# First batch of a graph-network kernel reordered: W ahead of the second adj, x in four buffers, c products behind W products

## The chip, the cores and the metric

One core of a Trainium2 chip runs the whole program. The metric is the device time of one execution in microseconds (us); lower is better. Each matmul engine (TensorE, PE), vector engine (VectorE, DVE), activation engine (ScalarE, ACT), GpSimd (POOL) and SyncE (SP, which issues every DMA here) runs its own list of instructions in program order; they wait for each other on semaphores.

## The reference, cut to what matters

For each of 16 batches x is 512 nodes by 128 features, adj is 512 by 512, and there are seven relations: adj twice, a node shift, the transposes of these three, and the identity.

```python
h = jnp.maximum(_layernorm(x, axis=-1), 0.0)
A_fwd = [A1, A2, shifted]
A_list = A_fwd + [jnp.swapaxes(a, 1, 2) for a in A_fwd]
A_list.append(eye)
A = jnp.stack(A_list, axis=0)
HW = jnp.einsum('bnf,rfo->rbno', features, W[:, :F]) + jnp.einsum('rd,rdo->ro', W_edges, W[:, F:])[:, None, None, :]
AHW = jnp.einsum('rbnm,rbmo->rbno', A, HW)
out = jnp.max(AHW, axis=0) + b
x = x + _L0_gnn_ref(h, adj, adj, L0_gnn_W, L0_gnn_W_edges, L0_gnn_b)
```

A1 and A2 are both adj. `shifted` rolls a stack of identities along its batch axis, which leaves each the identity, so relations 2, 5 and 6 act on h as it is. In the kernel they are the products of h with W (H_RELS), relations 3 and 4 the products with gT (AT_RELS), and 0 and 1 the products with g (A_RELS).

## The kernel before, in words

Everything is held transposed, 128 features or outputs on the partitions and 512 nodes along the row. Per batch b the kernel

- takes the statistics of x and makes rstd and shift on DVE (`variance`, `scale_and_shift`) and h on ACT (`make_h`, L387);
- multiplies h with adj and with its transpose, both loaded from memory, into the PSUM banks bank_gT (`aggregate_T`, L673 to L682) and bank_g (`aggregate`, L691 to L699). Two of four chunks are plain fp32; for the other two, adj is split into a high part (ACT, L358, L371) and a low part (DVE, `a_lo` L504, `aT_lo` L511);
- turns h and the row sums of adj on PE (`turn_h` L640, `turn_sums` L648). The sums come from ACT's accumulators and go through POOL (`part_sums`, L282, L286);
- splits gT, hT and g into high parts (ACT) and low parts (DVE, L527, L522, L532);
- makes seven products with W, each in three passes, high by high, low by high and high by low (`product`, L736 to L738). Products 3 to 6 start from the product of the row sums with c, the relations' constant rows (`begin_products`, L714, here called the c products);
- takes the maximum over the seven: ACT begins it (`begin_best`), DVE takes six more (`take_best`, L545 for products 1 and 2, L548 for 3 to 6);
- adds x and bias on POOL (`add_bias` L295, "x+bias" in the prediction; `finish` L303) and stores.

W is split once: high parts in two casts on DVE (products 0 to 2 L577, products 3 to 6 L593), low parts on POOL (L322, L325). `NH` is 3, the number of h products.

All tiles of a batch are double-buffered, x too. The order of the work is written out by hand on each engine. DVE in batch b goes through: variance of b+2, aT_lo of b, shift of b+1, a_lo of b+1, gT_lo, hT_lo, h_lo of b+1, g_lo, six bests. In batch 0 this row stands apart (L590 to L602). SP issues all DMAs from one queue: in the loop over b first x of b+2, then adj of b+2, the store of b-1, adjT and xT of b+2. Loads into a buffer in use wait for its last reader:

```python
            def load_x(b):
                q = b % 2
                if b >= 2:
                    sp.wait_ge(h_ready, b - 1)
```

PE goes through batch 0 in lines L740 to L757 and through the others in L758 to L767. The first product of a batch waits for hT_lo, the third for the copied row sums, the c products for g_lo, `aggregate` for the last best of the batch before (its bank_g is read there).

Of the kernel before, what the change touches and what calls it, by code (L numbers as in the profile page):

```python
# [11 lines left out]
P = 128  # L12
# [13 lines left out]
WARM_UP = 10  # L26


def gnn_kernel(nc: bass.Bass, x: bass.AP, xT: bass.AP, adj: bass.AP, adjT: bass.AP, W: bass.AP,
# [14 lines left out]
    with ExitStack() as ctx:  # L44
# [13 lines left out]
        x_sb = pair("x_sb", [P, C, F])  # L58
# [3 lines left out]

# [8 lines left out]
        aT_lo = pair("aT_lo", [P, NS, N], F32R)  # L71
        summed = pair("summed", [P, 2, C, N], mybir.dt.bfloat16)
# [54 lines left out]
        x_in = [sem(f"x_in{i}") for i in range(2)]  # L127
# [73 lines left out]
        def _(sp):  # L201
            def load_x(b):
                q = b % 2
                if b >= 2:
                    sp.wait_ge(h_ready, b - 1)
                    sp.wait_ge(h0_scaled, 1)
                sp.dma_start(x_sb[q][:, :, :], x_dram[b]).then_inc(x_in[q], 16)
# [36 lines left out]
            for c in range(C):  # L244
                sp.dma_start(adjT_sb[0][:, c, :], adjT_dram[0][:, c, :]).then_inc(adjT0_in[c], 16)
                if c == 1:
                    sp.dma_start(w_sb[:, 0:1, :], w_dram[:, 2:3, :]).then_inc(wh_in, 16)
                    sp.dma_start(w_sb[:, 1:3, :], w_dram[:, 5:7, :]).then_inc(wh_in, 16)
            load_x(1)
            load_adj(1)  # L250
            sp.dma_start(w_sb[:, 3:5, :], w_dram[:, 3:5, :]).then_inc(wa_in, 16)
            sp.dma_start(w_sb[:, 5:7, :], w_dram[:, 0:2, :]).then_inc(wa_in, 16)
            load_adjT(1)
            sp.dma_start(bias_sb[:, :], biasT).then_inc(bias_in, 16)
            load_xT(0)
# [18 lines left out]
        def _(pool):  # L274
# [66 lines left out]
        def _(act):  # L341
# [290 lines left out]
        def _(pe):  # L632
# [70 lines left out]
            def begin_products(b):  # L703
# [4 lines left out]
                for i in range(NH, NPROD - int(b == B - 1)):  # L708
                    begin_product(i, bank_of[i])

            def begin_product(i, to, nodes=slice(0, N)):
                group = ORDER_A.index(ORDER[i])
                rows = slice(group * GROUP, (group + 1) * GROUP)
                nc.tensor.matmul(to[:, nodes], c_rows[rows, :], sumsT[rows, nodes], start=True, stop=False)  # L714

            def product(b, i, nodes=slice(0, N), to=None):
                r = ORDER[i]
                dst = (to or bank_of[i])[:, nodes]
# [8 lines left out]
                if i == 3:  # L727
                    pe.wait_ge(gTlo_ready, b + 1)
                    pe.wait_ge(wlo_ready, 2)
                if r in H_RELS:  # L730
                    hi, lo = hT_hi, hT_lo
                elif r in AT_RELS:
                    hi, lo = gT_hi, gT_lo
                else:
                    hi, lo = g_hi, g_lo
                nc.tensor.matmul(dst, w_hi[:, i, :], hi[:, nodes], start=(r in H_RELS), stop=False)  # L736
                nc.tensor.matmul(dst, w_lo[:, i, :], hi[:, nodes], start=False, stop=False)  # L737
                nc.tensor.matmul(dst, w_hi[:, i, :], lo[:, nodes], start=False, stop=True).then_inc(prod_psum, 1)  # L738
# [12 lines left out]
            for i in range(NH):  # L751
                if i == 2:
                    turn_sums(0)
                product(0, i)
            begin_products(0)
            for i in range(NH, NPROD):
                product(0, i)  # L757
# [11 lines left out]
            for nodes, to in zip(HALVES, last_banks):  # L769
                begin_product(NPROD - 1, to, nodes)  # L770
# [28 lines left out]
```

## Time and profile before

| | us |
|---|---|
| median of 3 runs | 230.85 |
| lowest and highest | 229.27, 233.23 |
| the profiled execution | 230.21 |
| its span, first to last instruction | 228.5 |

The profile shows when each instruction ran in one execution. PE is the matmul engine; PEclk is the clock granted to it in tenths of full speed, where 5 is 1.2 GHz and 10 (shown as 9) is 2.4 GHz. Ends of matmuls are modelled: consecutive matmuls overlap in the listing, and their starts tell the pace. An instruction's idle time before it stands in brackets with what released it; "issue" means that nothing the profile shows was waited for.

### The profile page before, as it was taken

To read this page: it belongs to the slowest core of one execution; us is meant where nothing else is said; L and a number is where in the kernel's file an instruction comes from. 1 tells how busy PE (TensorE), PEld (TensorE's weight loads), DVE (VectorE), ACT (ScalarE), POOL (GpSimd) and SP (SyncE) were. 2 spreads that over 40 slices of the span, in tenths; PEclk is the share of its full clock that TensorE was granted. 3 is DMA by queue.
4 is the path that set the end of the run, shared out by engine and by line. 5 is a ranking of instruction groups with operands and counts; after the bars stand their busy time and mean duration, and the time that the engine had idled before them with its cause. 6 is when DMAs were issued, how large, how long until landed. Compare 5 with 4: busy or idle time off the path is not lost.

```text
span 228.5 us, 3306 instructions
## 1 busy us (share of the span) xinstructions
PE 213.9 (94%) x872; PEld 145.1 (63%) x872; DVE 172.2 (75%) x414; ACT 159.0 (70%) x431; POOL 57.8 (25%) x109
## 2 busy tenths in 40 slices
PE   7973799999999899999999999999999998999994
PEld 7532466667676567667667667677666665667672
DVE  3453987697876887897779788797778869787845
ACT  3756928778686777969586877969686867966220
POOL 3106322303232231213223231213223231223200
PEclk9997589999999999999999999999999999999999
DMA  5999907759293955949393866939393966610101
GB/s 184 310 355 371 336 5 243 265 192 303 44 382 103 313 185 200 308 100 331 114 346 127 264 241 209 295 123 348 88 333 123 306 202 238 221 46 3 47 0 46
DMA packets 31586, 47.13 MB, mean 206 GB/s; under 512 B 1632, under 2 KB 11088, under 8 KB 31568
## 3 DMA queue, kind: packets, MB, share of 16 engines
q1 hardware_dynamic: 31568, 46.92, 61.4%
q8 instruction: 7, 0.11, 0.2%
q14 instruction: 11, 0.09, 0.1%
HBM read 42.72 MB, written 4.19 MB: 205 GB/s over the span
## 4 chain that ended last, share of the span: by engine, by line
PE 85%; SPq 5%; DMA 4%; DVE 2%; issue 2%; DVEq 0%
PE bank_g L691 12%; PE bank_p L736 12%; PE bank_gT L673 11%; PE bank_p L738 10%; PE bank_p L737 10%; DMA x_sb<-in_x_dram 4%; PE bank_p L714 3%; PE bank_g L695 3%; PE bank_gT L678 3%; PE bank_gT L679 3%; PE bank_g L696 3%; PE bank_g L699 3%; PE bank_gT L682 3%; PE bank_p L640 3%; PE bank_p L648 3%
## 5 line engine op out<-in xcount | busy, mean ns | idle before, releaser
L548 DVE TENSOR_TENSOR best<-bank_p,best 128x512 f32<-128x512 f32 x48 | 33.2, 692 | 9.1 <-PE bank_p L738 8.1
L295 POOL TENSOR_TENSOR x_bias<-xT_sb,bias_sb 128x512 f32<-128x512 f32 x16 | 20.7, 1294 | 73.7 <-DVE h_lo L517 72.1
L403 ACT ACTIVATE gT_hi<-bank_gT 128x512 fp32r<-128x512 f32 x16 | 9.6, 598 | 37.5 <-PE bank_gT L682 37.1
L691 PE MATMUL bank_g<-adjT_sb,h 128*128 128x512 f32 x60 | 29.0, 605 | 0.0
L545 DVE SCALAR_TENSOR_TENSOR best<-bank_p,c_col,best 128x512 f32<-128x512 f32 x32 | 24.0, 751 | 6.4 <-ACT best L422 5.7
L387 ACT ACTIVATE h<-x_sb,shift,rstd 128x128 f32<-128x128 f32 x60 | 24.7, 491 | 5.9 <-DVE shift L497 5.9
L673 PE MATMUL bank_gT<-adj_sb,h 128*128 128x512 f32 x60 | 28.2, 592 | 0.0
L303 POOL TENSOR_TENSOR o_sb<-best,x_bias 128x512 f32<-128x512 f32 x15 | 19.8, 1320 | 28.2 <-DVE best L548 28.2
L479 DVE BATCH_NORM_STATS2 stats<-x_sb 128x6 f32<-128x128 f32 x64 | 14.0, 281 | 16.4 <-DMA x_sb<-in_x_dram 16.4
L736 PE MATMUL bank_p<-hT_hi,w_hi 128*128 128x512 f32 x48 | 20.1, 419 | 4.0 <-issue 2.9
L511 DVE TENSOR_TENSOR aT_lo<-adjT_sb,aT_hi 128x512 fp32r<-128x512 f32 x30 | 21.8, 767 | 0.0
L504 DVE TENSOR_TENSOR a_lo<-adj_sb,a_hi 128x512 fp32r<-128x512 f32 x30 | 19.3, 684 | 0.0
L737 PE MATMUL bank_p<-hT_hi,w_lo 128*128 128x512 f32 x48 | 19.2, 400 | 0.0
L738 PE MATMUL bank_p<-hT_lo,w_hi 128*128 128x512 f32 x48 | 19.2, 400 | 0.0
L358 ACT ACTIVATE a_hi<-adj_sb 128x512 fp32r<-128x512 f32 x30 | 18.5, 619 | 0.0
L374 ACT ACTIVATE summed<-adjT_sb 128x512 bf16<-128x512 f32 x30 | 18.5, 618 | 0.0
L371 ACT ACTIVATE aT_hi<-adjT_sb 128x512 fp32r<-128x512 f32 x30 | 18.5, 619 | 0.0
L361 ACT ACTIVATE summed<-adj_sb 128x512 bf16<-128x512 f32 x30 | 18.4, 617 | 0.0
L695 PE MATMUL bank_g<-aT_hi,h_hi 128*128 128x512 f32 x30 | 17.9, 596 | 0.0
L678 PE MATMUL bank_gT<-a_hi,h_hi 128*128 128x512 f32 x30 | 17.8, 595 | 0.0
L532 DVE TENSOR_TENSOR g_lo<-bank_g,g_hi 128x512 fp32r<-128x512 f32 x16 | 11.0, 690 | 8.6 <-ACT g_hi L409 8.6
L673 PEld LDWEIGHTS bank_gT<-adj_sb,h 128*128 128x128 f32 x60 | 11.4, 190 | 8.5 <-issue 7.2
(107 smaller groups left out, 470.2 us busy)
## 6 DMA issues: line engine op xcount, KB each, us to landing
adj_sb<-in_adj_dram SPq DMA_DIRECT2D x15, 1024.0 KB, 5.4
adjT_sb<-in_adjT_dram SPq DMA_DIRECT2D x15, 1024.0 KB, 5.8
xT_sb<-in_xT_dram SPq DMA_DIRECT2D x16, 256.0 KB, 6.1
x_sb<-in_x_dram SPq DMA_DIRECT2D x15, 256.0 KB, 6.4
out_dram<-o_sb SPq DMA_DIRECT2D x15, 256.0 KB, 6.0
adj_sb<-in_adj_dram SPq DMA_DIRECT2D x4, 256.0 KB, 3.8
adjT_sb<-in_adjT_dram SPq DMA_DIRECT2D x4, 256.0 KB, 4.4
w_sb<-in_W_dram SPq DMA_DIRECT2D x3, 128.0 KB, 7.0
```

Of the source, the lines that this page charges most:

```text
L295: nc.gpsimd.tensor_tensor(x_bias[q][:, :], xT_sb[q][:, :], bias_sb[:, :], ALU.add).then_inc(xb_ready, 1)
L387: last = nc.scalar.activation(h[q][:, c, :], x_sb[q][:, c, :], ACT.Relu, bias=shift[:, c:c + 1], scale=rstd[:, c:c + 1])
L511: nc.vector.tensor_tensor(aT_lo[q][:, i, :], adjT_sb[q][:, c, :], aT_hi[q][:, i, :].bitcast(F32), ALU.subtract).then_inc(aTlo_ready, 1)
L545: op = nc.vector.scalar_tensor_tensor(out=best[q][:, :], in0=product, scalar=c_col[:, r:r + 1], in1=best[q][:, :], op0=ALU.add, op1=ALU.max)
L548: op = nc.vector.tensor_tensor(best[q][:, :], product, best[q][:, :], ALU.max)
L673: nc.tensor.matmul(bank_gT[:, 0:N], h[q][:, c, :], adj_sb[q][:, c, :], start=(c == WHOLE[0]), stop=False)
L678: nc.tensor.matmul(bank_gT[:, 0:N], h_hi[q][:, i, :], a_hi[q][:, i, :], start=False, stop=False)
L691: nc.tensor.matmul(bank_g[:, 0:N], h[q][:, c, :], adjT_sb[q][:, c, :], start=(c == WHOLE[0]), stop=False)
L695: nc.tensor.matmul(bank_g[:, 0:N], h_hi[q][:, i, :], aT_hi[q][:, i, :], start=False, stop=False)
L736: nc.tensor.matmul(dst, w_hi[:, i, :], hi[:, nodes], start=(r in H_RELS), stop=False)
L737: nc.tensor.matmul(dst, w_lo[:, i, :], hi[:, nodes], start=False, stop=False)
L738: nc.tensor.matmul(dst, w_hi[:, i, :], lo[:, nodes], start=False, stop=True).then_inc(prod_psum, 1)
```

## The change

Four edits, all around the first batches:

1. SP: W's parts and x of batch 1 are issued ahead. x of batch 1 goes ahead of three pieces of the first adjT, the second half of W ahead of adj of batch 1, x of batch 2 ahead of bias and xT.
2. x has NX = 4 buffers. In the loop SP issues x of batch b+3, not of b+2.
3. PE: in batch 0 the W products 3 and 4 come between the turning of the sums and product 2, and the c products come last and end the accumulation of products 3 to 6.
4. DVE and POOL: in batch 0 DVE takes g_lo and the first best ahead of h_lo and the variance of batch 2; POOL makes W's second low part in two halves, one on either side of the row-sum parts.

```diff
-        x_sb = pair("x_sb", [P, C, F])
+        x_sb = [sb(f"x_sb{i}", [P, C, F]) for i in range(NX)]
...
+        def x_loads(b):
+
+            return 16 * (b // NX + int(b % NX > 0))
...
             def load_x(b):
-                q = b % 2
-                if b >= 2:
-                    sp.wait_ge(h_ready, b - 1)
+                q = b % NX
+                if b >= NX:
+                    sp.wait_ge(h_ready, b - NX + 1)
                     sp.wait_ge(h0_scaled, 1)
...
             for c in range(C):
                 sp.dma_start(adjT_sb[0][:, c, :], adjT_dram[0][:, c, :]).then_inc(adjT0_in[c], 16)
-                if c == 1:
+                if c == 0:
                     sp.dma_start(w_sb[:, 0:1, :], w_dram[:, 2:3, :]).then_inc(wh_in, 16)
                     sp.dma_start(w_sb[:, 1:3, :], w_dram[:, 5:7, :]).then_inc(wh_in, 16)
-            load_x(1)
-            load_adj(1)
+                    load_x(1)
             sp.dma_start(w_sb[:, 3:5, :], w_dram[:, 3:5, :]).then_inc(wa_in, 16)
             sp.dma_start(w_sb[:, 5:7, :], w_dram[:, 0:2, :]).then_inc(wa_in, 16)
+            load_adj(1)
             load_adjT(1)
+            load_x(2)
...
             for b in range(B):
+                if b + 3 < B:
+                    load_x(b + 3)
                 if b + 2 < B:
-                    load_x(b + 2)
                     load_adj(b + 2)
...
             pool.wait_ge(whi_ready, 2)
-            nc.gpsimd.tensor_tensor(w_lo[:, NH:, :], w_sb[:, NH:, :], w_hi[:, NH:, :].bitcast(F32),
+            nc.gpsimd.tensor_tensor(w_lo[:, NH:NH + 2, :], w_sb[:, NH:NH + 2, :], w_hi[:, NH:NH + 2, :].bitcast(F32),
                                     ALU.subtract).then_inc(wlo_ready, 1)
             pool.wait_ge(parts_zeroed, 1)
             part_sums(0)
+            nc.gpsimd.tensor_tensor(w_lo[:, NH + 2:, :], w_sb[:, NH + 2:, :], w_hi[:, NH + 2:, :].bitcast(F32),
+                                    ALU.subtract).then_inc(wlo_ready, 1)
...
             scale_and_shift(1)
+            split_g_lo(0)
+            take_best(0, 1)
+            split_h_lo(1)
             variance(2)
-            split_g_lo(0)
-            split_h_lo(1)
-            take_best(0, 1)
             take_best(0, 2)
...
+            def products_first():
+
+                product(0, 0)
+                product(0, 1)
+                turn_sums(0)
+                pe.wait_ge(gTlo_ready, 1)
+                pe.wait_ge(wlo_ready, 2)
+                passes(3, bank_of[3][:, 0:N], start=True)
+                passes(4, bank_of[4][:, 0:N], start=True)
+                product(0, 2)
+                pe.wait_ge(crow_ready, 1)
+                pe.wait_ge(wlo_ready, 3)
+                pe.wait_ge(glo_ready, 1)
+                passes(5, bank_of[5][:, 0:N], start=True)
+                passes(6, bank_of[6][:, 0:N], start=True)
+                for i in range(NH, NPROD):
+                    add_sums(i, bank_of[i], stop=True).then_inc(prod_psum, 1)
```

`passes` holds the three matmuls of a W product, `add_sums` the c product; both are what `product` and `begin_product` held before.

SP's queue behind the first adj, in the kernel before (the number behind a tile is its buffer; adj_sb0 and x_sb0 at the end of the piece are those of batch 2):

```order
L245 DMA adjT_sb0<-in_adjT_dram 128x512 x2
L207 DMA x_sb1<-in_x_dram 128x4x128
L216 DMA adj_sb1<-in_adj_dram 128x4x512
L251 DMA w_sb<-in_W_dram 128x2x128
L252 DMA w_sb<-in_W_dram 128x2x128
L225 DMA adjT_sb1<-in_adjT_dram 128x4x512
L254 DMA bias_sb<-in_biasT_dram 128x512
L231 DMA xT_sb0<-in_xT_dram 128x512
L231 DMA xT_sb1<-in_xT_dram 128x512
L207 DMA x_sb0<-in_x_dram 128x4x128 [waits h0_scaled,h_ready]
L216 DMA adj_sb0<-in_adj_dram 128x4x512 [waits gT_psum,sums_ready]
```

and in the changed kernel:

```order
L212 DMA x_sb1<-in_x_dram 128x4x128
L250 DMA adjT_sb0<-in_adjT_dram 128x512 x3
L255 DMA w_sb<-in_W_dram 128x2x128
L256 DMA w_sb<-in_W_dram 128x2x128
L221 DMA adj_sb1<-in_adj_dram 128x4x512
L230 DMA adjT_sb1<-in_adjT_dram 128x4x512
L212 DMA x_sb2<-in_x_dram 128x4x128
L260 DMA bias_sb<-in_biasT_dram 128x512
L236 DMA xT_sb0<-in_xT_dram 128x512
L236 DMA xT_sb1<-in_xT_dram 128x512
L212 DMA x_sb3<-in_x_dram 128x4x128
L221 DMA adj_sb0<-in_adj_dram 128x4x512 [waits gT_psum,sums_ready]
```

x of batch 1 moved ahead of three adjT pieces, W ahead of adj, and x of batch 2 ahead of bias and xT without a wait; x of batch 3 is new in this place.

DVE's row from the shift of batch 1 to the end of batch 0's bests, before:

```order
L497 SCALAR_TENSOR_TENSOR shift<-mean_var1,rstd 128x4 [waits rstd_ready]
L479 BN_STATS stats<-x_sb0 128x6 [waits x_in0]
L479 BN_STATS stats<-x_sb0 128x6 x3
L484 MEMSET wait_carrier 128x1 [waits std_ready,stats_done]
L486 BN_AGGR mean_var0<-stats 128x2 x4
L532 TENSOR_TENSOR g_lo<-bank_g,g_hi 128x512 [waits ghi_ready]
L517 TENSOR_TENSOR h_lo1<-h1,h_hi1 128x256 [waits hhi_ready]
L545 SCALAR_TENSOR_TENSOR best0<-bank_p1,c_col,best0 128x512 [waits prod_psum,best_begun]
L545 SCALAR_TENSOR_TENSOR best0<-bank_p2,c_col,best0 128x512 [waits prod_psum,best_done]
L504 TENSOR_TENSOR a_lo1<-adj_sb1,a_hi1 128x512 [waits ahi_ready] x2
```

and changed:

```order
L506 SCALAR_TENSOR_TENSOR shift<-mean_var1,rstd 128x4 [waits rstd_ready]
L541 TENSOR_TENSOR g_lo<-bank_g,g_hi 128x512 [waits ghi_ready]
L554 SCALAR_TENSOR_TENSOR best0<-bank_p1,c_col,best0 128x512 [waits prod_psum,best_begun]
L526 TENSOR_TENSOR h_lo1<-h1,h_hi1 128x256 [waits hhi_ready]
L488 BN_STATS stats<-x_sb2 128x6 [waits x_in2]
L488 BN_STATS stats<-x_sb2 128x6 x3
L493 MEMSET wait_carrier 128x1 [waits std_ready,stats_done]
L495 BN_AGGR mean_var0<-stats 128x2 x4
L554 SCALAR_TENSOR_TENSOR best0<-bank_p2,c_col,best0 128x512 [waits prod_psum,best_done]
L513 TENSOR_TENSOR a_lo1<-adj_sb1,a_hi1 128x512 [waits ahi_ready] x2
```

g_lo, the first best and h_lo now stand ahead of the statistics of batch 2, which wait for x.

PE in batch 0, from the turning of the sums on, changed (before, product 2 and the four c products stood where products 3 and 4 stand now):

```order
L657 MATMUL bank_p2<-ident_r,sum_parts0 128x128 [waits parts_lo]
...
L733 MATMUL bank_p3<-gT_hi,w_hi 128x512 [waits wlo_ready,gTlo_ready]
...
L733 MATMUL bank_p4<-gT_hi,w_hi 128x512
...
L733 MATMUL bank_p2<-hT_hi,w_hi 128x512 [waits sumsT_ready]
...
L733 MATMUL bank_p5<-g_hi,w_hi 128x512 [waits glo_ready,wlo_ready,crow_ready]
...
L733 MATMUL bank_g<-g_hi,w_hi 128x512
...
L723 MATMUL bank_p3<-sumsT,c_rows 128x512
```

Only the first pass of each product is shown. The wait for g_lo stands behind three products, and the c products are last.

## Rows read from the trace of the kernel before

**Rows 1.** The page: span, busy time, two groups of instructions, granted clock in 40 slices

```profile
span 228.5 us, 3306 instructions
PE 213.9 (94%) x872; PEld 145.1 (63%) x872; DVE 172.2 (75%) x414; ACT 159.0 (70%) x431; POOL 57.8 (25%) x109
...
PEclk9997589999999999999999999999999999999999
...
L548 DVE TENSOR_TENSOR best<-bank_p,best 128x512 f32<-128x512 f32 x48 | 33.2, 692 | 9.1 <-PE bank_p L738 8.1
...
L545 DVE SCALAR_TENSOR_TENSOR best<-bank_p,c_col,best 128x512 f32<-128x512 f32 x32 | 24.0, 751 | 6.4 <-ACT best L422 5.7
```

**Rows 2.** Chain of waits in order of time (start us, us, what)

```profile
14.16 8.59 DMA x_sb<-in_x_dram
...
26.31 0.43 PE bank_p L737
...
38.17 0.24 PE bank_p L737
```

**Rows 3.** DVE's timeline, batches 0 and 1 (start us, us, what, idle before)

```profile
17.12 0.43 DVE L593 CAST w_hi<-w_sb 128x512 fp32r<-128x512 f32 x1 [1.93 <-DMA w_sb<-in_W_dram]
...
17.67 1.24 DVE L497 SCALAR_TENSOR_TENSOR shift<-mean_var,rstd 128x4 f32<-128x4 f32 x1
22.77 0.87 DVE L479 BATCH_NORM_STATS2 stats<-x_sb 128x6 f32<-128x128 f32 x4 [3.87 <-DMA x_sb<-in_x_dram]
...
23.98 0.66 DVE L532 TENSOR_TENSOR g_lo<-bank_g,g_hi 128x512 fp32r<-128x512 f32 x1
...
26.34 1.28 DVE L504 TENSOR_TENSOR a_lo<-adj_sb,a_hi 128x512 fp32r<-128x512 f32 x2
...
31.56 0.86 DVE L479 BATCH_NORM_STATS2 stats<-x_sb 128x6 f32<-128x128 f32 x4
...
36.22 0.68 DVE L522 TENSOR_TENSOR hT_lo<-bank_p,hT_hi 128x512 fp32r<-128x512 f32 x1
```

**Rows 4.** PE's timeline, 0 to 50 us

```profile
19.75 0.66 PE L648 MATMUL bank_p<-ident_r,sum_parts 128*128 128x128 f32 x4 [3.79 <-POOL sum_parts L286]
...
24.79 0.79 PE L714 MATMUL bank_p<-sumsT,c_rows 32*128 32x512 f32 x3 [1.57 <-DVE g_lo L532]
...
30.68 1.88 PE L673 MATMUL bank_gT<-adj_sb,h 128*128 128x512 f32 x4
...
37.78 0.39 PE L736 MATMUL bank_p<-hT_hi,w_hi 128*128 128x512 f32 x1
...
43.30 1.88 PE L673 MATMUL bank_gT<-adj_sb,h 128*128 128x512 f32 x4
```

**Rows 5.** Window 19 to 20 us: busy by engine, then PEclk, DMA share, GB/s

```profile
19.00:20.00 1.00, 0.25 (x2) 0.26 (x3) 0.00 (x0) 1.00 (x3) 0.61 (x4) 1.00 1.06 372
```

**Rows 6.** Timelines of DVE and PE, a later batch and the last

```profile
72.26 0.87 DVE L479 BATCH_NORM_STATS2 stats<-x_sb 128x6 f32<-128x128 f32 x4 [1.96 <-DMA x_sb<-in_x_dram]
...
77.52 0.47 PE L736 MATMUL bank_p<-hT_hi,w_hi 128*128 128x512 f32 x1 [0.99 <-issue]
...
211.48 1.88 PE L673 MATMUL bank_gT<-adj_sb,h 128*128 128x512 f32 x4
```

**Rows 7.** Who waited for whom after 46 us (us in total, times, longest)

```profile
DVE stats L479 <- DMA x_sb<-in_x_dram: 10.4, 10, 2.0
```

**Rows 8.** POOL's timeline, 17 to 24 us

```profile
17.62 1.26 POOL L325 TENSOR_TENSOR w_lo<-w_sb,w_hi 128x512 fp32r<-128x512 f32 x1 [6.17 <-DVE w_hi L593]
...
21.30 2.51 POOL L295 TENSOR_TENSOR x_bias<-xT_sb,bias_sb 128x512 f32<-128x512 f32 x2 [1.61 <-DMA xT_sb<-in_xT_dram]
```

**Rows 9.** ACT's timeline, end of the passes over adj of batch 2

```profile
29.43 0.20 ACT L361 ACTIVATION_READ_ACCUMULATOR summed<-adj_sb 128x1 f32 x1
```

**Rows 10.** Timelines of DVE and POOL near the end

```profile
212.44 2.38 DVE L511 TENSOR_TENSOR aT_lo<-adjT_sb,aT_hi 128x512 fp32r<-128x512 f32 x2
...
212.69 1.58 POOL L303 TENSOR_TENSOR o_sb<-best,x_bias 128x512 f32<-128x512 f32 x1 [1.77 <-DVE best L548]
```

More of the change, by code:

```diff
@@ L26 @@
 WARM_UP = 10
+NX = 4
 def gnn_kernel(nc: bass.Bass, x: bass.AP, xT: bass.AP, adj: bass.AP, adjT: bass.AP, W: bass.AP,
@@ L126, in gnn_kernel @@
         x0_in = [sem(f"x0_in{i}") for i in range(2)]
-        x_in = [sem(f"x_in{i}") for i in range(2)]
+        x_in = [sem(f"x_in{i}") for i in range(NX)]
         xT_in = [sem(f"xT_in{i}") for i in range(2)]
@@ L386, in make_h @@
                 for c in range(C):
-                    last = nc.scalar.activation(h[q][:, c, :], x_sb[q][:, c, :], ACT.Relu,
+                    last = nc.scalar.activation(h[q][:, c, :], x_sb[b % NX][:, c, :], ACT.Relu,
                                                 bias=shift[:, c:c + 1], scale=rstd[:, c:c + 1])
@@ L477, in variance @@
                     elif b > 0 and c == 0:
-                        dve.wait_ge(x_in[q], times(b))
-                    last = nc.vector.bn_stats(stats[:, c, :], x_sb[q][:, c, :])
+                        dve.wait_ge(x_in[b % NX], x_loads(b))
+                    last = nc.vector.bn_stats(stats[:, c, :], x_sb[b % NX][:, c, :])
                 last.then_inc(stats_done, 1)
@@ L708, in begin_products, with add_sums, passes @@
                 for i in range(NH, NPROD - int(b == B - 1)):
-                    begin_product(i, bank_of[i])
-            def begin_product(i, to, nodes=slice(0, N)):
+                    add_sums(i, bank_of[i], start=True)
+            def add_sums(i, to, nodes=slice(0, N), start=False, stop=False):
                 group = ORDER_A.index(ORDER[i])
                 rows = slice(group * GROUP, (group + 1) * GROUP)
-                nc.tensor.matmul(to[:, nodes], c_rows[rows, :], sumsT[rows, nodes], start=True, stop=False)
+                return nc.tensor.matmul(to[:, nodes], c_rows[rows, :], sumsT[rows, nodes], start=start, stop=stop)
+            def passes(i, dst, nodes=slice(0, N), start=False, stop=False):
+                r = ORDER[i]
+                if r in H_RELS:
+                    hi, lo = hT_hi, hT_lo
+                elif r in AT_RELS:
+                    hi, lo = gT_hi, gT_lo
+                else:
+                    hi, lo = g_hi, g_lo
+                nc.tensor.matmul(dst, w_hi[:, i, :], hi[:, nodes], start=start, stop=False)
+                nc.tensor.matmul(dst, w_lo[:, i, :], hi[:, nodes], start=False, stop=False)
+                return nc.tensor.matmul(dst, w_hi[:, i, :], lo[:, nodes], start=False, stop=stop)
             def product(b, i, nodes=slice(0, N), to=None):
-                r = ORDER[i]
-                dst = (to or bank_of[i])[:, nodes]
                 if i == 0:
@@ L728, in product @@
                     pe.wait_ge(gTlo_ready, b + 1)
[L729 to L738, printed above, removed]
+                passes(i, (to or bank_of[i])[:, nodes], nodes, start=ORDER[i] in H_RELS,
+                       stop=True).then_inc(prod_psum, 1)
+            def products_first():
[14 more added lines that the diff above has]
+                    add_sums(i, bank_of[i], stop=True).then_inc(prod_psum, 1)
             pe.wait_ge(ident_ready, 1)
@@ L750, in _ @@
             pe.wait_ge(identr_ready, 1)
[L751 to L757, printed above, removed]
+            products_first()
             for b in range(1, B):
@@ L769, in _ @@
             for nodes, to in zip(HALVES, last_banks):
-                begin_product(NPROD - 1, to, nodes)
+                add_sums(NPROD - 1, to, nodes, start=True)
                 product(B - 1, NPROD - 1, nodes, to)
```

## The prediction

> **What bounds the kernel now.** I read the page first. TensorE (PE) is busy 94% of the 228.5 us, and its granted clock falls to half in a stretch of the first 35 us only [rows 1]. So PE sets the time, and there are two questions: where does PE stand idle or run at half speed, and who lets it go again.
>
> The chain of waits answers the first one: its only long step that is not PE work is a transfer of x of 8.59 us, from 14.16 to 22.75 [rows 2]. That is x of batch 2, for which VectorE (DVE) waits 3.87 us before its statistics; the low part of g for batch 0 stands behind them in DVE's row and starts only at 23.98 [rows 3]. PE's timeline of the same stretch has three holes: 3.79 us before the turning of the row sums at 19.75 (released by GpSimd, POOL), then one for their copy, then 1.57 us before the c products at 24.79 (released by g_lo) [rows 4]. Until 20 us the granted clock is 1.00 [rows 5]; the page's slices of 5.7 us then show 0.7, 0.5 and 0.8 [rows 1], so it is at half, 1.2 GHz, for some 10 us after the first hole, and a pass of a W product takes 0.43 us there for 0.24 later [rows 2]. Batch 1 starts at 30.68 [rows 4].
>
> From there every undisturbed batch takes 43.30 - 30.68 = 12.62 us on PE [rows 4]. Fourteen of them would end at 30.68 + 176.7 = 207.4, but the last batch starts at 211.48 [rows 6]. So 4.1 us are lost later. One such place is in view: DVE waits 1.96 us for x at 72.26, and PE's first W product of that batch is 0.99 us late [rows 6]. The two fit: in batch 1 the low part of hT, for which that product waits, ends at 36.22 + 0.68 = 36.9 [rows 3], and PE wants it at 37.78 [rows 4]. DVE has 0.9 us to spare, and a wait of 1.96 leaves 1.06. In all there are 10 such waits with 10.4 us [rows 7].
>
> **The start: W and x earlier.** DVE waits 1.93 us for the second part of W until 17.12, and behind its cast stand rstd and shift of batch 1, which end at 17.67 + 1.24 = 18.9 [rows 3]; POOL's W low part (1.26 us) and the row-sum parts stand behind it too, and PE's 3.79 us behind those [rows 4, 8]. Now W's second part is issued ahead of the 1 MB adj of batch 1. At 372 GB/s [rows 5] that is 2.8 us earlier, and x of batch 1 going ahead of three adjT pieces gives nothing back before the same bytes have passed: W at about 14.3 at the latest. The cast then follows DVE's earlier work at 14.5 to 14.9. The POOL part before the row sums is half as wide (0.6 to 0.7 us for 1.26), so the parts are there at 14.9 + 0.7 + 0.9 = 16.5 for 19.7. PE, free at 15.96 [rows 4], stands 0.6 to 1 us and not 3.79, and keeps the full clock. Its remaining batch-0 work is 0.4 (turning, an estimate from its row of 0.66 with the overlap off), five products of three passes, 0.7 each, and the c products, some 0.6 at full clock (0.79 for each at half, started together [rows 4]): 4.5 us, with the small gaps 5. Product 2 waits for the copied sums, but two W products are now ahead of it; products 3 to 6 no longer wait for g_lo and the sums at once. Batch 1 starts near 21.7: 9 us earlier than at 30.68.
>
> **What is late next.** That gain can't be kept, since DVE follows. I go down DVE's row of the changed kernel. x of batch 2 now lands ahead of bias and two xT, 786 kB; at 372 GB/s 2.1 us sooner: 22.75 - 2.1 = 20.65. Then, without a pause:
> variance of batch 2, 1.2 (22.77 to 23.98) [rows 3], until 21.85; the second best, 0.75 [rows 1], until 22.6; the two a_lo, 1.28 [rows 3], until 23.9; four bests of 0.69 [rows 1], until 26.7; then the same block that in the kernel before runs from 31.56 to 36.9, statistics of batch 3 to hT_lo [rows 3], 5.3 us, until 32.0.
> PE wants hT_lo of batch 1 at 21.7 + 7.1 = 28.8. So DVE decides and PE waits, some of it earlier already (the aggregate with adjT waits for the last best, 26.7). The other candidate is ScalarE (ACT): adj of batch 2, 1 MB behind x of batch 2, came at 22.75 + 2.8 = 25.6 by the same rate and has x of batch 3 ahead of it now, 0.7 us; ACT's four passes over it, 0.6 each and done at 29.63 before [rows 9], then end at 28.8, and gT and hT are copied by about 29.8. DVE comes later, ACT adds nothing.
>
> **A collision on the way.** POOL's two x+bias sums run for 1.25 us each from 21.30 on, when DVE does single-input work [rows 8, 3]. Now the first starts 0.7 us later (one 256 KB transfer more ahead), 22.0 to 23.25, and the first a_lo wants to start at 22.6. What two SBUF-reading instructions do to each other is seen in two places. The shift of batch 1 took 1.24 us beside W's low part on POOL (17.62 to 18.88), and a pair of aT_lo took 2.38 for 1.28 where POOL's output sum started 0.25 after its first one, while that sum took 1.58 [rows 3, 8, 10]: they go in turns. In turns means here: a_lo waits 0.65, runs to 23.9, the second x+bias runs to 25.15, the second a_lo to 25.8, 1.9 us later than 23.9. Bounds: 0 (no overlap) and 1.9. I take 1.9, since the order of arrival (x, bias, xT) fixes the overlap, and both rows show the full price.
> The Trainium skill (SBUF — State Buffer, "Who interferes with whom") says the same: a DVE instruction with two SBUF inputs and a GpSimd one that reads SBUF exclude each other for a whole instruction, the first to start wins. It speaks against this change, and the rows above agree with it. By the rule hT_lo comes at 33.9; if only GpSimd had to give way it would be 32.0.
>
> So product 0 of batch 1 starts at about 34.0, and not at 37.78: **3.8 us gained**; some 5 of the 9 go back as PE waits.
>
> **Four x buffers.** x of batch b+3 is now issued where x of batch b+2 stood, so it has a whole batch (12.6 us) more for a transfer that was at most 2.0 us late [rows 7]. The bytes are the same. The waits of x go; with them the 4.1 us of later batches, if DVE was the cause in all of them. The cover for what remains is the 0.9 us of slack; aT_lo will now meet POOL's output sum in every batch, as it did in batch 1 (that cost is inside the 36.9). Bounds: 0 and 4.1. I take **4.1**, because the one place worked out fits to 0.1 us.
>
> The c products behind the W products in batch 0 are the same four instructions; the pass from 32 rows to 128 rows is still made once. The split of POOL's W part adds one instruction, after the sums, under PE's work. SP (the DMA queue) is moved past nothing that it had to wait for: x of batch 3 has its own buffer now.
>
> **Sum.** 228.5 - 3.8 - 4.1 = 220.6 span. The profiled execution took 230.21, 1.71 more than its span, so **222.3 us**. Its 230.21 is 0.3% under the median 230.85; 2%, about what a measurement of this kernel tells from no change, is 4.6 us.
>
> **Rivals.**
> 1. No collision: x+bias and a_lo miss each other, or DVE gets in first. 1.9 less, 220.4. For it: transfer times of 0.5 us decide who starts first. Against: the order. 0.17.
> 2. The clock falls again. PE stands idle in batch 1 three times (about 1.4 before the end of gT, 1.5 for the last best, 2.1 for hT_lo). Before, it fell after holes of 3.79 and more, and not for the later hole of 0.99 [rows 4, 6]. If a stretch like the one before (some 10 us, 5.5 us of full-speed work) comes over batch 1 and 2, it costs 4.5, less what the waits cover: 225 to 227. The Trainium skill (TensorE: Matmul & The Clock Gate, Part 1: The HAM clock gate) lets the clock be halved when the array is idle and restored under work, as the granted clock here shows; by it the three holes are a risk, and the single hole of batch 0 is gone. 0.15.
> 3. The x waits were not what delayed PE later, or another wait (ACT's g copy, adj landing) takes their place: 3.8 gained only, 226.4. For it: I worked through one batch. 0.11.
> 4. The start gives nothing: W does not come sooner, or the DVE row ends as late as before; then 4.1 remain, 226.1. 0.04.
> 5. Slower than before. The mechanism is the clock of rival 2 that does not come back, since each new hole renews it: work at half clock takes 1.82 times as long (0.43 for 0.236 a pass). The 7.9 us gained are lost once 9.7 us of full-speed PE work, about three quarters of a batch, run so; two batches would cost 20.7 us, 243. Against: PE has no hole after batch 1 with x there in time. 0.03.
>
> **How the numbers follow.** Forecast 0.50, rivals 0.17, 0.15, 0.11, 0.04, 0.03. The likeliest case alone spans 220.9 to 223.8 (1 us of x's landing each way, and part of the collision). The range 219.4 to 226.2 takes in rival 1 with some of the ACT slack, most of 2, and the edge of 3 and 4. Faster by over 2% means under 226.2: forecast and rival 1 wholly, most of 2, half of 3 and 4: 0.81. Within 2%: 0.16. Slower: 0.03.
>
> **What would show it.** W's second cast at about 14.5; PE's first hole under 1 us and the granted clock at 1.00 from 20 to 30; first matmul of batch 1 near 22, of batch 2 near 39.5, then every 12.6 us; a_lo of batch 1 stretched from 1.28 to over 3 us beside the x+bias sums; no DVE wait for x after batch 1. Wrong it is if batch 2 starts after 42, if the clock shows a stretch at half speed after 21 us, or if later batches still differ by up to 1 us on PE.

## The result, and the profile after

The changed kernel takes 221.77 us (median of 4 executions, 221.73 to 222.47); the kernel before, 230.21 (4 executions, 229.27 to 233.23). The ratio is 0.9654, with a 95% interval of 0.9604 to 0.9703. Forecast were 222.3 us.

The page of the changed kernel, the same lines as in [rows 1] (span, busy time, granted clock, bests), and the lines of the aT_lo and a_lo groups:

```profile
span 220.0 us, 3290 instructions
...
PE 209.7 (95%) x872; PEld 143.1 (65%) x872; DVE 175.3 (80%) x414; ACT 159.0 (72%) x431; POOL 58.5 (27%) x110
...
PEclk9999999999999999999999999999999999999999
...
L557 DVE TENSOR_TENSOR best<-bank_p,best 128x512 f32<-128x512 f32 x48 | 33.2, 691 | 8.2 <-PE bank_p L735 7.2
...
L520 DVE TENSOR_TENSOR aT_lo<-adjT_sb,aT_hi 128x512 fp32r<-128x512 f32 x30 | 24.1, 842 | 0.0
...
L513 DVE TENSOR_TENSOR a_lo<-adj_sb,a_hi 128x512 fp32r<-128x512 f32 x30 | 21.1, 746 | 0.0
```

PE is busy 4.2 us less than before (209.7 for 213.9), although it does the same matmuls: the dip in the granted clock is gone. DVE is busy 3.1 us more, and it is instructions that met POOL: a_lo takes 1.8 us more than before (21.1 for 19.3), all of it in batch 1, and aT_lo 2.3 more (24.1 for 21.8), since its pair now takes 1.49 us beside POOL's output sum where it took 1.26 in the batches in which DVE had waited for x. The shift of batch 1 gives 0.5 back.

PE's timeline of the changed kernel, against [rows 4] and the last line of [rows 6]:

```profile
16.45 0.66 PE L657 MATMUL bank_p<-ident_r,sum_parts 128*128 128x128 f32 x4 [0.47 <-POOL sum_parts L293]
...
21.04 1.98 PE L682 MATMUL bank_gT<-adj_sb,h 128*128 128x512 f32 x4
...
25.37 0.50 PE L691 MATMUL bank_gT<-a_lo,h_hi 128*128 128x512 f32 x1 [1.18 <-DVE a_lo L513]
...
28.24 1.96 PE L700 MATMUL bank_g<-adjT_sb,h 128*128 128x512 f32 x4 [1.49 <-DVE best L557]
...
33.46 0.47 PE L733 MATMUL bank_p<-hT_hi,w_hi 128*128 128x512 f32 x1 [1.87 <-issue]
...
39.06 1.88 PE L682 MATMUL bank_gT<-adj_sb,h 128*128 128x512 f32 x4
...
203.04 1.88 PE L682 MATMUL bank_gT<-adj_sb,h 128*128 128x512 f32 x4
```

Batch 1 starts at 21.04 for 30.68, then PE stands three times, and batch 2 starts at 39.06 for 43.30. Of 9.6 us won, 5.4 are given back in one batch. From there to the last batch it is 163.98 us, 13 times 12.61; before it was 211.48 - 43.30 = 168.18. The account of the span: 4.24 up to batch 2, 4.20 after it, 0.06 at the end, together the 8.5 us of 228.5 - 220.0.

DVE's timeline of the same stretch, against [rows 3], and POOL's, against [rows 8]:

```profile
14.35 0.42 DVE L602 CAST w_hi<-w_sb 128x512 fp32r<-128x512 f32 x1
...
14.89 0.72 DVE L506 SCALAR_TENSOR_TENSOR shift<-mean_var,rstd 128x4 f32<-128x4 f32 x1
...
20.33 0.87 DVE L488 BATCH_NORM_STATS2 stats<-x_sb 128x6 f32<-128x128 f32 x4 [0.41 <-DMA x_sb<-in_x_dram]
...
22.17 3.14 DVE L513 TENSOR_TENSOR a_lo<-adj_sb,a_hi 128x512 fp32r<-128x512 f32 x2
...
28.02 0.86 DVE L488 BATCH_NORM_STATS2 stats<-x_sb 128x6 f32<-128x128 f32 x4
...
32.67 0.68 DVE L531 TENSOR_TENSOR hT_lo<-bank_p,hT_hi 128x512 fp32r<-128x512 f32 x1
```

```profile
14.85 0.74 POOL L332 TENSOR_TENSOR w_lo<-w_sb,w_hi 128x256 fp32r<-128x256 f32 x1 [3.68 <-DVE w_hi L602]
...
21.81 2.96 POOL L302 TENSOR_TENSOR x_bias<-xT_sb,bias_sb 128x512 f32<-128x512 f32 x2 [4.73 <-DMA xT_sb<-in_xT_dram]
```

From 20.33 to 33.35 DVE has no pause, and its wait of 0.41 us for x at 20.33 is the last one for x. The a_lo pair takes 3.14 us for 1.28, and the two x+bias sums beside it 2.96 for 2.51. PE's product 0 follows 0.1 us behind hT_lo.

### The profile page after: what moved, and what is told of

The parts are those of the page before. It is cut to its first block, busy times and chain, and to the rows that moved or that the text cites. A ratio compares the mean times of both kernels' runs of the same rounds, so it can differ in the third digit from the quotient of the medians.

```text
span 220.0 us, 3290 instructions
## 1 busy us (share of the span) xinstructions
PE 209.7 (95%) x872; PEld 143.1 (65%) x872; DVE 175.3 (80%) x414; ACT 159.0 (72%) x431; POOL 58.5 (27%) x110
## 4 chain that ended last, share of the span: by engine, by line
PE 83%; DMA 5%; DVE 4%; SPq 4%; issue 2%; DVEq 0%
PE bank_g L700 12%; PE bank_gT L682 11%; PE bank_p L733 11%; PE bank_p L734 9%; PE bank_p L735 9%; DMA x_sb<-in_x_dram 5%; PE bank_g L704 3%; PE bank_g L708 3%; PE bank_g L705 3%; PE bank_gT L687 3%; PE bank_gT L688 3%; PE bank_p L723 3%; PE bank_gT L691 3%; PE bank_p L649 3%; PE bank_p L657 3%
## 5 line engine op out<-in xcount | busy, mean ns | idle before, releaser
L302 POOL TENSOR_TENSOR x_bias<-xT_sb,bias_sb 128x512 f32<-128x512 f32 x16 | 21.1, 1322 | 72.2 <-DVE h_lo L526 67.5
L520 DVE TENSOR_TENSOR aT_lo<-adjT_sb,aT_hi 128x512 fp32r<-128x512 f32 x30 | 24.1, 842 | 0.0
L733 PE MATMUL bank_p<-hT_hi,w_hi 128*128 128x512 f32 x48 | 19.4, 404 | 1.9 <-issue 1.9
L513 DVE TENSOR_TENSOR a_lo<-adj_sb,a_hi 128x512 fp32r<-128x512 f32 x30 | 21.1, 746 | 0.0
L700 PEld LDWEIGHTS bank_g<-adjT_sb,h 128*128 128x128 f32 x60 | 10.2, 191 | 8.8 <-issue 8.8
```

The costliest lines, as they stand in the source:

```text
L302: nc.gpsimd.tensor_tensor(x_bias[q][:, :], xT_sb[q][:, :], bias_sb[:, :], ALU.add).then_inc(xb_ready, 1)
L520: nc.vector.tensor_tensor(aT_lo[q][:, i, :], adjT_sb[q][:, c, :], aT_hi[q][:, i, :].bitcast(F32), ALU.subtract).then_inc(aTlo_ready, 1)
L700: nc.tensor.matmul(bank_g[:, 0:N], h[q][:, c, :], adjT_sb[q][:, c, :], start=(c == WHOLE[0]), stop=False)
L733: nc.tensor.matmul(dst, w_hi[:, i, :], hi[:, nodes], start=start, stop=False)
```

## The experiments

Every kernel ran beside the kernel before, and each ratio is to that kernel on the same chip (its medians there were 229.6 to 230.3 us). The changed kernel itself was measured in the first comparison only, on its own. Each interval reaches about 1 us to either side, so where two experiments differ by 1 us the place in the trace carries the argument.

### Four x buffers alone

The kernel before with NX = 4 buffers and

```diff
             load_xT(1)
+            load_x(2)
             for b in range(B):
+                if b + 3 < B:
+                    load_x(b + 3)
                 if b + 2 < B:
-                    load_x(b + 2)
                     load_adj(b + 2)
```

> The kernel before with four x buffers and x of batch b+3 issued in the loop, nothing else changed. My theory (DVE's waits for x cost PE 4.1 us after batch 2, and the buffers alone remove them): batch 1 starts at 30.7 as before, every later batch takes 12.62 us, no DVE wait for x after batch 2, and 230.2 - 4.1 = 226.1 us. Rival (the late batches of before had another cause, or the gain needs the new start): 230 us, batches between 12.6 and 13.9.

Measured: 225.33 us (224.43 to 225.76), ratio 0.9800 (0.9744 to 0.9857), 4.3 us under the kernel before beside it (229.63). In the profiled execution batch 1 starts at 30.37, batch 2 at 42.98 and every one after it 12.61 or 12.62 later. PE's timeline, a later batch and the last two:

```profile
42.98 1.88 PE L680 MATMUL bank_gT<-adj_sb,h 128*128 128x512 f32 x4
...
194.38 1.88 PE L680 MATMUL bank_gT<-adj_sb,h 128*128 128x512 f32 x4
207.00 1.88 PE L680 MATMUL bank_gT<-adj_sb,h 128*128 128x512 f32 x4
```

From 42.98 to 207.00 is 164.02 for the 168.18 of before: the 4.1 us were the x waits, and the buffers need nothing of the new start. DVE's last wait for x is the one for batch 2.

This also prices a late x. DVE's and PE's timelines of the kernel before, a short wait and a long one:

```profile
97.44 0.87 DVE L479 BATCH_NORM_STATS2 stats<-x_sb 128x6 f32<-128x128 f32 x4 [0.65 <-DMA x_sb<-in_x_dram]
...
187.99 0.87 DVE L479 BATCH_NORM_STATS2 stats<-x_sb 128x6 f32<-128x128 f32 x4 [1.69 <-DMA x_sb<-in_x_dram]
```

```profile
185.25 1.88 PE L673 MATMUL bank_gT<-adj_sb,h 128*128 128x512 f32 x4
...
198.86 1.88 PE L673 MATMUL bank_gT<-adj_sb,h 128*128 128x512 f32 x4
```

The batch with the wait of 0.65 us takes 12.63 us, like the four others with waits of 0.46 to 0.64. The one with 1.69 takes 13.61, 0.99 too much. All five long waits (1.11 to 1.96 us) cost their length less 0.70 to 0.72, together 4.1 us.

### The start alone

The changed kernel with two buffers, the loop's x loads as before:

```diff
-NX = 4
+NX = 2
...
-                if b + 3 < B:
-                    load_x(b + 3)
+                if 0 < b < B - 2:
+                    load_x(b + 2)
                 if b + 2 < B:
```

> The changed kernel with two x buffers: the new start of SP, DVE, POOL and PE, the loop's x loads as in before. If the two halves of the change simply add: 230.2 - 4.2 = 226.0, batch 2 starts at 39.1. My theory says they don't: x of batch 3 is then issued behind xT of batch 2, lands near 29.5 to 30 as before, and DVE wants it at 28.0, so hT_lo of batch 1 and the start of batch 2 come 1.5 to 2 us later (41), and the x waits of later batches are back (4.2): 227.5 to 228 us.

Measured: 226.83 us (225.67 to 228.05), ratio 0.9869 (0.9806 to 0.9931), between the two forecasts. DVE's and PE's timelines of the profiled execution (228.05 us, the longest of the six):

```profile
29.48 0.87 DVE L488 BATCH_NORM_STATS2 stats<-x_sb 128x6 f32<-128x128 f32 x4 [1.62 <-DMA x_sb<-in_x_dram]
...
34.73 0.47 PE L733 MATMUL bank_p<-hT_hi,w_hi 128*128 128x512 f32 x1 [2.23 <-issue]
...
165.34 0.47 PE L733 MATMUL bank_p<-hT_hi,w_hi 128*128 128x512 f32 x1 [1.17 <-issue]
```

The wait for x of batch 3 is there (1.62 us), product 0 is 1.27 later than with four buffers, and the late holes are back. Something I had not put into the forecast came on top: behind the hole of 2.23 us the granted clock is 0.61, 0.50, 0.50 and 0.68 in the four microseconds from 36 to 40, and batch 2 starts at 41.81. By the medians of that comparison the two halves save 4.3 and 2.8 us, together 7.1; the whole change saves 7.9 against the same 229.63. The interplay is seen in the trace; in the medians it is inside the noise.

### POOL out of the way of a_lo

```diff
-            add_bias(0)
-            add_bias(1)
             for b in range(1, B):
                 part_sums(b)
+                if b == 1:
+                    add_bias(0)
+                    add_bias(1)
                 finish(b - 1)
```

> The changed kernel, with POOL's two x+bias sums behind the row-sum parts of batch 1 and not ahead of them. Theory (the 3.14 us of the first a_lo pair are POOL's doing): the pair takes 1.28 us again, DVE's row after it is 1.86 earlier, 0.7 of it is lost again because POOL's output sum of batch 0 starts later and meets the whole of the first aT_lo: hT_lo of batch 1 ends near 32.2 for 33.35, 220.5 us. Rival (the pair was slow by itself or PE has another limit right behind): no change, 221.8. Rival 2 (the later xT load holds up SP's queue): x, adj of batches 3 and 4 late, over 221.8.

Measured: 221.02 us (220.37 to 221.94), ratio 0.9624 (0.9578 to 0.9670). DVE's timeline, then PE's:

```profile
21.96 1.28 DVE L514 TENSOR_TENSOR a_lo<-adj_sb,a_hi 128x512 fp32r<-128x512 f32 x2
...
27.13 2.15 DVE L521 TENSOR_TENSOR aT_lo<-adjT_sb,aT_hi 128x512 fp32r<-128x512 f32 x2
...
31.29 0.68 DVE L532 TENSOR_TENSOR hT_lo<-bank_p,hT_hi 128x512 fp32r<-128x512 f32 x1
```

```profile
32.07 0.47 PE L734 MATMUL bank_p<-hT_hi,w_hi 128*128 128x512 f32 x1 [2.24 <-issue]
...
34.27 0.63 PE L735 MATMUL bank_p<-hT_hi,w_lo 128*128 128x512 f32 x1
```

The second of PE's rows is a pass of a W product, and it takes 0.63 us where the listing has 0.40 at full clock. Two windows of one us say why (busy by engine, then granted clock, DMA share, GB/s):

```profile
34.00:35.00 1.00, 1.00 (x4) 0.50 (x2) 0.75 (x1) 1.00 (x5) 0.00 (x0) 0.50 1.04 401
35.00:36.00 1.00, 1.00 (x6) 0.31 (x5) 0.57 (x1) 1.00 (x4) 0.00 (x0) 0.50 1.06 410
```

The pair is back at 1.28 us without any other change to it, so its 3.14 was POOL's doing. The 0.7 us lost at aT_lo (2.15 for 1.46) came as forecast, and hT_lo ends at 31.97, 1.38 earlier. Yet in this execution batch 2 starts at 39.17, no earlier than in the changed kernel: from 33.3 to 36.6 us a pass takes 0.43 and not 0.24 us, which costs 1.5. Two of the six executions show it so (spans 220.2, mean clock 0.992); the four with a mean clock of 0.999 or 1.0 have spans of 218.6 to 219.4, against 219.9 and 220.0 in the two executions of the changed kernel with a mean clock of 1.0. So the collision costs about 1 us, and the clock can take it back. The two kernels ran in different comparisons, so this 1 us is an estimate.

The Trainium skill (SBUF — State Buffer, "Who interferes with whom") has the rule that a DVE instruction with two SBUF inputs contends with a GpSimd instruction that reads SBUF. The traces agree: 3.14 us with the overlap, 1.28 without.

### PE's order of before

```diff
-            products_first()
+            for i in range(NH):
+                if i == 2:
+                    turn_sums(0)
+                product(0, i)
+            pe.wait_ge(wlo_ready, 3)
+            begin_products(0)
+            for i in range(NH, NPROD):
+                product(0, i)
```

> The changed kernel with PE's batch 0 in the order of before (product 2 right behind the turning, c products ahead of the W products 3 to 6). Theory (PE waits for DVE in batch 1 anyway): a new hole of some 1.3 us before product 2 and one of a few tenths more, batch 1 starts near 22.4 for 21.04, and all of it is taken from PE's waits in batch 1: batch 2 starts at 39.1 as in the changed kernel, 221.8 us. Rival (the c products' place is worth its hole): 223 us. Second rival (the granted clock falls again): over 224.

Measured: 223.22 us (221.69 to 224.41), ratio 0.9707 (0.9654 to 0.9760), 1.4 over the changed kernel (1.2 by the ratios, whose intervals overlap). My theory missed. PE's timeline, the hole, the middle of the clock's first fall, batch 1, the second fall, batch 2:

```profile
18.02 0.51 PE L733 MATMUL bank_p<-hT_hi,w_hi 128*128 128x512 f32 x1 [1.16 <-ACT sumsT L424]
...
20.64 0.63 PE L734 MATMUL bank_p<-gT_hi,w_lo 128*128 128x512 f32 x1
...
23.73 1.88 PE L682 MATMUL bank_gT<-adj_sb,h 128*128 128x512 f32 x4
...
34.02 0.47 PE L733 MATMUL bank_p<-hT_hi,w_hi 128*128 128x512 f32 x1 [1.86 <-issue]
...
35.94 0.63 PE L734 MATMUL bank_p<-hT_hi,w_lo 128*128 128x512 f32 x1
...
41.09 1.88 PE L682 MATMUL bank_gT<-adj_sb,h 128*128 128x512 f32 x4
```

The hole of 1.16 us is as forecast. What I took for unlikely happened: the clock fell behind it (0.69, 0.50, 0.50 and 0.60 in the four microseconds from 18 to 22), though it is a third of the hole that brought it down before, and once more behind the hole of 1.86. The part of the theory that said PE waits for DVE anyway holds: batch 1 starts 2.7 us later (23.73), product 0 of it only 0.56 (34.02 for 33.46), and that much x of batch 2 landed later in this execution (DVE took it up at 20.88). The second fall lies where nothing covers it: from product 0 to batch 2 it is 7.07 us for 5.60. All six executions have a mean clock of 0.992 or 0.985. The profiled one, with two falls, has 0.985; one fall of this length leaves 0.992 (the third experiment's trace has one and 0.992). So the five others have about one fall each, and which of the two it is their means don't tell. In the changed kernel two of four executions are below 1.0.

### W behind adj, and DVE's order of before

```diff
+            load_adj(1)
             sp.dma_start(w_sb[:, 3:5, :], w_dram[:, 3:5, :]).then_inc(wa_in, 16)
             sp.dma_start(w_sb[:, 5:7, :], w_dram[:, 0:2, :]).then_inc(wa_in, 16)
-            load_adj(1)
```

> The changed kernel with the second half of W again behind adj of batch 1. Theory (PE and DVE are in series at the start, so only what delays hT_lo of batch 1 counts): the cast is back at 17.1, PE's first hole is over 3 us and the clock falls there, but most of the delay vanishes in PE's later waits: hT_lo of batch 1 ends near 35.2 for 33.35, 223.5 to 224 us. Rival (W's place is the whole gain of the start): 226 us.

Measured: 223.47 us (222.86 to 225.04), ratio 0.9747 (0.9689 to 0.9805). The cast is at 17.25, the hole 3.57 us, hT_lo ends at 34.95 (forecast 35.2). PE starts batch 1 at 25.45, 4.4 us later than the changed kernel; batch 2 starts at 40.65, 1.6 later. DVE's timeline:

```profile
22.39 1.50 DVE L526 TENSOR_TENSOR h_lo<-h,h_hi 128x256 fp32r<-128x256 f32 x1
...
25.64 1.28 DVE L513 TENSOR_TENSOR a_lo<-adj_sb,a_hi 128x512 fp32r<-128x512 f32 x2
```

And DVE's order of before:

```diff
+            variance(2)
             split_g_lo(0)
-            take_best(0, 1)
             split_h_lo(1)
-            variance(2)
+            take_best(0, 1)
             take_best(0, 2)
```

> The changed kernel with DVE's row of before: variance of batch 2 ahead of g_lo, h_lo and the first best. Theory: g_lo comes at 21.5 to 22.1, PE has a hole of some 3 us before product 5 and its clock falls to half for some us; DVE's row loses 0.7 to 1.1 us in all, since most of what it put off is done in time it waited for anyway: 222.4 to 223 us. Rival (the hole on PE counts whole): 224.8 us.

Measured: 222.85 us (222.29 to 223.21), ratio 0.9703 (0.9659 to 0.9746). The hole before product 5 is 3.39 us and the clock is at half from about 23.6 to 27; batch 1 starts at 26.02, 5.0 us later, and batch 2 at 40.44, 1.4 later. DVE's timeline:

```profile
22.76 1.27 DVE L526 TENSOR_TENSOR h_lo<-h,h_hi 128x256 fp32r<-128x256 f32 x1
...
25.39 1.33 DVE L513 TENSOR_TENSOR a_lo<-adj_sb,a_hi 128x512 fp32r<-128x512 f32 x2
```

Both say the same: a delay of 4 to 5 us at the start of batch 1 comes to 1.4 to 1.6 at the start of batch 2, and DVE's row tells why. The a_lo pair starts 3.5 and 3.2 us later than in the changed kernel (22.17), in the first because W's late cast made the first best late, in the second because g_lo, h_lo and the first best now stand between x's statistics and it. Then it takes 1.28 and 1.33 us and not 3.14, since POOL's sums met h_lo instead (1.50 and 1.27 us for 0.41): 1.9 and 1.8 us come back. So the delay of DVE's row counts in full, and it is small only because the collision moved. What a delay of PE alone is worth, the run with PE's order of before says: batch 1 2.7 us later, product 0 not later than x of batch 2 explains.

### x of batch 2 early

If DVE's row from x of batch 2 on sets the start, it should begin earlier. DVE waited 2.63 us ahead of the first best in the changed kernel.

```diff
+            load_x(2)
             load_adj(1)
             load_adjT(1)
-            load_x(2)
...
             split_g_lo(0)
+            variance(2)
             take_best(0, 1)
             split_h_lo(1)
-            variance(2)
             take_best(0, 2)
```

> The changed kernel, x of batch 2 issued ahead of both matrices of batch 1, and its variance on DVE ahead of the first best, where DVE waited 2.6 us. Theory (DVE's row from x of batch 2 on sets the start): the row begins 1.6 us earlier, the a_lo pair ends before the x+bias sums begin (1.28 again), hT_lo of batch 1 ends near 30.4 for 33.35; 218.8 us if the granted clock holds, up to 1.5 more if PE's longer hole before product 0 of batch 1 brings it down. Rival (ACT behind adj of batch 2 sets the end): gT_hi not before 29, hT_lo at 32 or later, 220.5 us or more.

Measured: 219.63 us (218.78 to 221.27), ratio 0.9571 (0.9529 to 0.9613): faster than both kernels, 2.1 us under the changed one, and 0.8 over the forecast. The changed kernel with filled holes, measured beside it (below), has no execution under 221.5; this one has none above 221.3. DVE's timeline, POOL's, then PE's:

```profile
16.45 0.86 DVE L488 BATCH_NORM_STATS2 stats<-x_sb 128x6 f32<-128x128 f32 x4
...
20.82 1.28 DVE L513 TENSOR_TENSOR a_lo<-adj_sb,a_hi 128x512 fp32r<-128x512 f32 x2
...
29.69 0.68 DVE L531 TENSOR_TENSOR hT_lo<-bank_p,hT_hi 128x512 fp32r<-128x512 f32 x1
```

```profile
21.43 3.07 POOL L302 TENSOR_TENSOR x_bias<-xT_sb,bias_sb 128x512 f32<-128x512 f32 x2 [4.03 <-DMA xT_sb<-in_xT_dram]
```

```profile
30.47 0.47 PE L733 MATMUL bank_p<-hT_hi,w_hi 128*128 128x512 f32 x1 [1.30 <-issue]
...
33.14 0.50 PE L723 MATMUL bank_p<-sumsT,c_rows 32*128 32x512 f32 x3 [0.32 <-DVE g_lo L541]
...
36.47 1.88 PE L682 MATMUL bank_gT<-adj_sb,h 128*128 128x512 f32 x4
```

The statistics no longer wait, and hT_lo ends at 30.37 (forecast 30.4). The pair doesn't end before POOL starts, as I had expected: it ends at 22.10 and POOL's sums start at 21.43. But DVE is in first, so here it is POOL that waits: its two sums take 3.07 us for 2.51, and the pair keeps its 1.28. Batch 2 starts 2.6 us earlier. Now ACT is next: h of batch 2 comes after its passes over adj of batch 2, h_lo and g_lo wait for it, and PE stands 0.32 us for g_lo.

### The holes filled

To see whether the holes bring the clock down, matmuls of the identity into a free bank stand in them; nobody reads the result. The diff shows the helper; it is called ahead of the waits.

```diff
+            def fill(n):
+                for _ in range(n):
+                    nc.tensor.matmul(bank_p[0][:, 0:P], ident[:, :], ident[:, :], start=True, stop=True)
```

> The changed kernel with matmuls of the identity that nobody reads (4, 6 and 8) in PE's three holes of batch 1. Theory (the spread between executions is the granted clock, which falls for some 3 us behind these holes in some of them): mean clock 1.0 in nearly every execution, batch 2 starts at 39.1 in all, 221.7 us, none above 222.2. Rival (the clock at the start has nothing to do with the holes): same spread, 221.7 to 222.5, with means of 0.985 to 1.0. If the filling is too long, batch 2 starts later than 39.1.

Measured: 221.64 us (221.52 to 222.11), ratio 0.9656 (0.9621 to 0.9690), mean clocks 0.996 to 1.0. PE's only hole left in batch 1 is 0.23 us, and batch 2 starts at 38.93. The changed kernel's four executions have means from 0.985 to 1.0. The time is the same and the spread hardly smaller (0.6 us for 0.7), so this run alone shows only that filling costs nothing.

The mean clock must be read with care, for it takes in the end of the span too. The profiled execution has 0.996, yet its granted clock is 1.00 in every window up to 218 us. PE's last matmul starts at 216.42, and the two windows behind it are the ones below 1.00:

```profile
218.00:219.00 1.00, 0.00 (x0) 0.00 (x0) 0.00 (x0) 0.00 (x0) 0.00 (x0) 0.60 0.57 193
219.00:220.00 1.00, 0.00 (x0) 0.00 (x0) 0.00 (x0) 0.00 (x0) 0.00 (x0) 0.50 0.01 3
```

So a mean of 0.996 or more is no sign of a fall during PE's work. A mean of 0.992 or less is one in every trace kept.

The same with x of batch 2 early (five matmuls ahead of product 0) and with the x+bias sums moved (4 and 10 matmuls):

> x of batch 2 early as in the run before, and five unread matmuls of the identity in PE's hole of 1.3 us ahead of product 0 of batch 1. Theory (the one execution at 221.27 was the granted clock): no execution above 220.3, median 219.3, batch 2 starts at 36.5. Rival (the spread of x-early is the landing of the loads): same spread, 218.8 to 221.3, with clock means of 1.0.

Measured: 219.56 us (219.04 to 220.26), ratio 0.9559 (0.9508 to 0.9611). None is above 220.3, as the theory had it; batch 2 starts at 37.08, not 36.5, since adj of batch 2 landed 0.6 us later in that execution and ACT with it (DVE waits 0.65 for gT_hi). The median is that of the kernel without filling.

> The x+bias sums behind the row-sum parts of batch 1, as in the third experiment, and PE's two holes of batch 1 filled with 4 and 10 unread matmuls. Theory (the collision's price of 1.2 to 1.4 us was there, and the half clock took it back in some executions): clock means of 0.995 or more, batch 2 starts near 37.7 for 39.17, median 220.4 us, 1.2 under the filled kernel with the collision (221.64). Rival (the collision costs nothing in the end): 221.6 us.

Measured: 220.64 us (220.41 to 222.53), ratio 0.9619 (0.9568 to 0.9671), 1.0 under the filled kernel with the collision. Batch 2 starts at 37.95 for 38.93 there. Five of six executions lie at 220.4 to 220.7; the sixth, at 222.53, has a mean clock of 0.995, between the two groups, and its cause stays open. Of the 18 executions of the three filled kernels none has a mean below 0.995; of the 16 of the same kernels unfilled, five have 0.985 to 0.992. So the holes have a part in the falls. In the medians filling gains nothing that can be told (221.64 for 221.77, 219.56 for 219.63, 220.64 for 221.02); the long executions of the last two kernels (221.3, and 221.9 twice) are gone, but there is the new one of 222.53.

## Why the prediction was right, point by point

- **What bounds the kernel; x waits worth 4.1.** Right: 4.20 in the trace of after, 4.16 with the buffers alone. The buffers alone took the waits and the 4.1 us away, so the cause is shown. The slack, though, was read too large: with 0.9 us the five long waits would have cost 3.2 us, and they cost 4.1, their length less 0.71 each. That the one worked place fitted to 0.1 us was luck: I set 1.06 beside PE's hole of 0.99, but that batch took 13.86 us, 1.24 too much. The 4.1 itself came from the starts of the batches and did not hang on it.
- **W earlier.** Cast at 14.35 (forecast 14.3 to 14.9), first hole 0.47 (0.6 to 1), batch 1 at 21.04 (21.7). Taken back alone, W's place costs 1.7 us in the medians (2.1 by the ratios), not the 4 it moves batch 1, because the a_lo pair then misses POOL's sums.
- **DVE's row.** x of batch 2 at 20.3 (20.65), the last block 28.02 to 33.35, 5.33 (5.3), product 0 of batch 1 at 33.46 (34.0): 4.3 us gained, not 3.8. Of the 0.5 us more, 0.3 is the earlier landing of x, the rest a slightly shorter row from there to the last best.
- **The collision.** 1.86 us more for the pair, forecast 1.9; rival 1 fell. But in the end its worth is about 1 us by the filled kernels and by the third experiment alike, not 1.9, since POOL's work meets aT_lo instead when it is moved. Its price in the row was right; as a bound for what could be won by avoiding it in this way it was too large.
- **ACT adds nothing.** Right for the changed kernel: gT_hi was copied by 29.02, and DVE came to it at 32.07. It is next once DVE is 3 us earlier.
- **The clock (rival 2, 0.15).** In the profiled execution it held. But the rival had more in it than I gave: I forecast one stretch of 10 us. What the runs show is stretches of 3 to 4 us behind holes of 1.2 to 2.2, in some executions and not in others, at about 1.5 us each where nothing covers them. That the clock "fell after holes of 3.79 and more" was too mild a reading: 1.16 is enough. The changed kernel did not escape it: by their mean clocks (0.985 and 0.99) two of its four executions have falls, yet they are only 0.7 us and nothing longer than the others. Presumably those falls lay in time in which PE waits for DVE anyway; no trace of them was kept. The prediction named such cover and still put rival 2 at 225 to 227 us. That falls could come in half of the executions and leave the median where it was, it did not foresee; there the forecast had luck.
- **The c products last.** I cost this at nothing by itself, with PE's wait as cover. The wait covers the hole, as forecast, but not the clock: in the medians PE's order is worth 1.2 to 1.4 us, inside the noise of two such comparisons. That run took back both the c products' place and product 2's, so what the c products' place is worth alone is not shown.
- **Rivals 3 and 4** (3.8 or 4.1 alone) fell by the first two experiments, each half giving its own part. Rival 5 has nothing for it.

## What to carry to other kernels

Where two engines hand work to each other at a start, find the row that has no pause up to the first steady stage; only what moves its beginning or its sum counts, and the gain of the other engine's earlier start is given back as waits (9.6 us became 4.2 here). Read the slack of one undisturbed period and compare the late arrivals with it, but check it on more than one of them, from the starts of the batches and not from the hole in brackets. Here 0.7 us of each long wait was covered and the rest was on the path, and the extra buffers gave it back (4.16 us for 4.11 lost). When an order is changed, look for what now runs at the same time on DVE and POOL: the overlap took 1.9 us here, nearly what x's earlier landing brought (2.4), and a change that delays the row can look cheap because it moves the overlap away.

## What the runs showed of the hardware

- The granted clock fell to half for 3 to 4 us behind holes in PE's work of 1.16 us (with 0.45 just before it) and 1.86 (PE's order of before), 2.23 (the start alone), 2.24 (POOL out of the way), 3.39 (DVE's order) and 3.57 (W behind adj). It did not fall behind 1.18, 1.49 and 1.87 in the trace of the changed kernel, nor behind 1.30 with x early and 1.87 with W behind adj. By the mean clocks the same program does both: 0.992 in two executions with POOL out of the way, 0.999 to 1.0 in four.
- A DVE subtraction with both inputs in SBUF and a POOL sum take turns: a pair of 1.28 us and a pair of 2.51 us became 3.14 and 2.96 side by side where POOL was first, 1.28 and 3.07 where DVE was first. With DVE's order of before it was h_lo that met the first of the two sums, and its 0.41 us became 1.27.
- The four c products, each on 32 rows of its own, start within 0.01 us in the listing and together take 0.43 us at full clock (20.61 to 21.04), less than two passes of a W product at 0.24 each.
